# Attention stage of a three-stage language-model kernel: adjoining pairs on TensorE, one exponential per two heads, q and k stacked together

## The chip, the cores and the metric

The kernel runs on one NeuronCore of a Trainium2 chip. The metric is the device time of one execution in microseconds. Three runs of the kernel before took 1275.78, 1275.93 and 1276.22 us (median 1275.93).

## The reference

Three models run one after the other over 2048 tokens (8 sequences of 256) of width 256: a tower of four state-space layers, then an attention with a distance kernel, then two layers of windowed attention. Only the second is touched. On h, the layer-normed output of the tower:

```python
qh = (q @ Wq).reshape(Bq, Sq, H, D).transpose(0, 2, 1, 3)      # H = 16 heads of D = 16; k and v alike
q_norm = jnp.sum(qh * qh, axis=-1, keepdims=True)
qk = jnp.einsum('bhsd,bhtd->bhst', qh, kh)
dist = jnp.maximum(q_norm - 2.0 * qk + jnp.swapaxes(k_norm, -2, -1), 0.0)
scores = jnp.exp(-gamma[None, :, None, None] * SCALE * dist)
scores = jnp.where(mask, scores, 0.0)                          # mask: strictly above the diagonal
out = jnp.einsum('bhst,bhtd->bhsd', scores, vh)
return out.transpose(0, 2, 1, 3).reshape(Bq, Sq, H * D) @ Wo
```

## The kernel before

The second stage (`attention_phase`) handles one sequence of 256 tokens (two tiles t of 128) at a time, eight in all, M = 8. Products of fp32 accuracy are made of high and low parts: an engine rounds a value to fp32r (`_hi`), another subtracts it from the value (`_lo`), and TensorE multiplies the parts.

For a sequence s the steps are these. VectorE takes statistics and applies them twice (`norm_stats`, `norm_apply`, with k = 0 for the tower's last norm and k = 1 for the attention's own); GpSimd raises the variance to the power -1/2 (`rstd`) and applies scale and bias (`scale_h`, `bias_h`). TensorE transposes (`turn_x`), ScalarE and VectorE split (`spread`, `split_x`), TensorE projects (`project_qk`, one tile each, and `project_v`). ScalarE squares, VectorE sums per head (`norms`), and the two write a stacked row of 64 per head and tile: high and low parts of q, of -2k and of the norms, so that one product of 64 rows gives the whole distance (`query_hi`, `key_hi` on ScalarE, `stack` on VectorE). TensorE turns the rows (`turn`, eight transposes of 128x128 for q or k of one tile), ScalarE and, for the keys of tile 0, VectorE copy them out (`turned_q`, `turned_k`).

Then come eight pairs of heads, numbered 0 to 7. For a pair c TensorE computes `distances` (L938 and L941, four matmuls) into two banks, VectorE clips them at 0 (`clip`, L1336), ScalarE takes the exponential, one instruction per head since each head has its own factor `gsc` (`kernel_exp`, L1178), GpSimd masks (`mask`, L1476). After two pairs TensorE multiplies with the values (`values`, L959 and L957, quads 0 to 3 for pairs 0-1, 2-3, 4-5 and 6-7). `output_hi`, `output_lo`, `project_out` and `add_output` end the sequence.

All this is a software pipeline written out by hand. Each engine has a function `half(h)`, which lists what it does for several sequences at once, in fixed order; an engine works its list strictly in order and waits on semaphores. TensorE's half handles sequences a = h (projections of q and k), b = h-1 (values' projection, turns, the first two distances), c = h-2 (the other distances, values) and d = h-3 (output). VectorE's and GpSimd's lists are offset: the same stretch of time is their half h+3. Halves 2 to 8 of TensorE work on this stage alone; before them `first` and behind them halves 9 and 10 work beside the third stage, whose own halves follow.

The eight PSUM banks are shared by hand. The argument b of a step names a pair of banks, 2b and 2b+1 (`ps[:, 2 * b, ...]`).

In GpSimd's list two lines matter here: `rstd(c, 1)` (L1458) stands between `mask(f, 6)` and `mask(f, 7)`, and it waits for the `norm_stats(c, 1)` of VectorE (L1272, L1278, L1281).

## Time and profile before

| what | value |
|---|---|
| median of three runs | 1275.93 us |
| the profiled execution, own time | 1278.31 us |
| its span in the profile | 1276.4 us |
| TensorE busy | 1209.8 us, 95% |
| VectorE, ScalarE, GpSimd busy | 984.7, 860.2, 621.2 us |
| granted TensorE clock, mean over the span | 0.983 |
| second stage in the span | about 517 to 670 us |

Busy is the time an engine executes instructions; a matmul's end is modelled, so that starts of TensorE's instructions are to be read rather than their ends. A start-to-start time of two instructions is the price in a row of them; an instruction's own duration is a little longer, since the next one begins before it ends.

### The profile page before, as it was taken

Reading aid. Unit: us, or ns where it says so; the run is one execution under the profiler, and the core shown is the slowest. Engines: PE = TensorE matmul, PEld = TensorE weight load, DVE = VectorE, ACT = ScalarE, POOL = GpSimd, SP = SyncE. Lnnn points to the kernel's source line nnn. Section 1 sums busy time; section 2 is a strip of 40 time slices with the busy share of each in tenths; the row PEclk is TensorE's granted clock in tenths of the full one; section 3 lists DMA queues with packets and bytes.
Section 4 is the critical chain, followed back from the end, with each engine's and each line's share of the span. In section 5 each row is a group of like instructions: output and inputs, shape, how many; then the busy total and the mean of one; then the engine's idle time right before and its main releaser. Section 6 shows DMA issues by size and latency. Waiting matters only on the chain.

```text
span 1276.4 us, 26138 instructions
## 1 busy us (share of the span) xinstructions
PE 1209.8 (95%) x8899; PEld 1028.5 (81%) x8899; DVE 984.7 (77%) x2624; ACT 860.2 (67%) x1989; POOL 621.2 (49%) x678
## 2 busy tenths in 40 slices
PE   5999999999999999799978799999999999999998
PEld 3799988988888989577756567888888888888898
DVE  5767676666667777789878988888888888888754
ACT  2455766675556556689964668778777777777764
POOL 6523441361145243455434568556655567556543
PEclk9899999999999999899989999999999999999999
DMA  7400010001000000300110002000100000000001
GB/s 172 115 2 15 2 66 0 14 33 33 0 8 1 1 1 1 77 10 18 58 54 17 1 5 95 6 5 6 48 3 6 22 6 13 22 17 18 22 10 42
DMA packets 39615, 33.25 MB, mean 26 GB/s; under 512 B 16774, under 2 KB 36178, under 8 KB 39506
## 3 DMA queue, kind: packets, MB, share of 16 engines
q1 hardware_dynamic: 38610, 29.74, 7.7%
q0 software_dynamic: 768, 2.10, 1.0%
q8 instruction: 60, 0.98, 0.3%
q14 instruction: 49, 0.40, 0.1%
q10 hardware_dynamic: 128, 0.04, 0.0%
HBM read 25.84 MB, written 4.19 MB: 24 GB/s over the span
## 4 chain that ended last, share of the span: by engine, by line
PE 45%; DVE 6%; issue 3%; POOL 2%; ACT 2%; DVEq 0%; ACTq 0%; POOLq 0%
PE w_ps_p L1914 3%; PE w_ring L1975 3%; PE w_ring L1976 3%; PE w_ring L1873 3%; PE w_ring L1977 3%; PE w_ring L1875 3%; PE w_ring L1874 3%; PE w_ps_a L1932 2%; PE w_ring L1987 2%; PE a_ps L925 2%; PE w_ps_d L1907 2%; PE w_ps_d L1904 2%; PE w_ring L1891 2%; PE w_ring L1988 2%; PE w_ring L1991 1%
## 5 line engine op out<-in xcount | busy, mean ns | idle before, releaser
L392 ACT ACTIVATE t_gf<-t_ps_f,t_fb_cur 128x512 f32<-128x512 f32 x128 | 87.9, 687 | 159.8 <-PE t_ps_f L298 156.6
L542 DVE TENSOR_TENSOR t_g_lo<-t_gf,t_g_hi 128x512 fp32r<-128x512 f32 x128 | 93.3, 730 | 69.3 <-ACT t_g_hi L394 68.9
L311 PE MATMUL t_ps_o<-t_w_hi,t_g_hi 128*128 128x256 f32 x512 | 144.6, 282 | 0.1
L312 PE MATMUL t_ps_o<-t_w_lo,t_g_hi 128*128 128x256 f32 x512 | 143.0, 279 | 0.0
L313 PE MATMUL t_ps_o<-t_w_hi,t_g_lo 128*128 128x256 f32 x512 | 142.9, 279 | 0.0
L695 POOL TENSOR_TENSOR t_rs<-t_ve,t_neghalf 128x4 f32<-128x4 f32 x32 | 40.9, 1277 | 159.8 <-DVE t_ve L503 158.2
L296 PE MATMUL t_ps_f<-t_nh,t_w_hi 128*128 128x512 f32 x256 | 102.6, 401 | 1.5 <-DVE t_nl L518 0.8
L2988 POOL TENSOR_TENSOR w_m<-w_m 128x512 f32<-128x512 f32 x64 | 84.2, 1316 | 36.9 <-DVE w_m L2631 36.8
L298 PE MATMUL t_ps_f<-t_nl,t_w_hi 128*128 128x512 f32 x256 | 100.3, 392 | 0.0
L297 PE MATMUL t_ps_f<-t_nh,t_w_lo 128*128 128x512 f32 x256 | 100.0, 391 | 0.0
L311 PEld LDWEIGHTS t_ps_o<-t_w_hi,t_g_hi 128*128 128x128 f32 x512 | 96.2, 188 | 4.1 <-issue 0.9
L312 PEld LDWEIGHTS t_ps_o<-t_w_lo,t_g_hi 128*128 128x128 f32 x512 | 96.7, 189 | 2.5
L313 PEld LDWEIGHTS t_ps_o<-t_w_hi,t_g_lo 128*128 128x128 f32 x512 | 96.8, 189 | 0.0
L2674 DVE COPY w_pt<-w_ps_p 128x384 f32<-128x384 f32 x128 | 70.5, 551 | 31.4 <-PE w_ps_p L1914 29.9
L1975 PE MATMUL w_ring<-w_nh,w_w_hi 128*128 128x256 f32 x318 | 93.5, 294 | 0.0
L1976 PE MATMUL w_ring<-w_nh,w_w_lo 128*128 128x256 f32 x318 | 88.8, 279 | 0.0
L1977 PE MATMUL w_ring<-w_nl,w_w_hi 128*128 128x256 f32 x318 | 88.7, 279 | 0.0
L2999 POOL TENSOR_TENSOR w_pr<-w_pr,w_rinv 128x256 f32<-128x256 f32 x64 | 39.3, 614 | 101.0 <-DVE w_rinv L2668 101.0
L1873 PE MATMUL w_ring<-qkv_hi,w_ah 128*128 128x512 f32 x188 | 80.6, 429 | 6.7 <-DVE w_al L2613 5.7
L3004 POOL TENSOR_TENSOR w_h_lo<-w_gate,w_h_hi 128x256 fp32r<-128x256 f32 x75 | 54.6, 737 | 60.1 <-ACT w_h_hi L2413 60.1
L394 ACT ACTIVATE t_g_hi<-t_gf 128x512 fp32r<-128x512 f32 x128 | 80.9, 632 | 4.1
L1178 ACT ACTIVATE a_e<-a_dist,a_gsc 128x384 f32<-128x384 f32 x128 | 70.2, 621 | 8.3 <-DVE a_dist L1336 6.8
(369 smaller groups left out, 4285.0 us busy)
## 6 DMA issues: line engine op xcount, KB each, us to landing
t_raw<-in_L_tok_w SPq DMA_DIRECT2D x8, 1024.0 KB, 5.4
out<-X SPq DMA_DIRECT2D x14, 256.0 KB, 2.2
raw<-in_L_ffn_wqkv SPq DMA_DIRECT2D x2, 1536.0 KB, 6.9
raw<-in_L_ffn_w SPq DMA_DIRECT2D x4, 640.0 KB, 4.8
w_raw_o<-out SPq DMA_DIRECT2D x8, 256.0 KB, 2.8
w_xs<-X SPq DMA_DIRECT2D x14, 127.0 KB
w_raw<-in_L_ffn_w SPq DMA_DIRECT2D x2, 640.0 KB
t_raw_d<-in_L_tok_D SPq DMA_DIRECT2D x4, 256.0 KB
```

The source lines that it names most:

```text
L296: pe.matmul(ps_f[:, j % 2, :], w1_hi[:, c, col], nh[1][:, c, :], start=(c == 0), stop=False)
L297: pe.matmul(ps_f[:, j % 2, :], w1_lo[:, c, col], nh[1][:, c, :], start=False, stop=False)
L298: mm = pe.matmul(ps_f[:, j % 2, :], w1_hi[:, c, col], nl[1][:, c, :], start=False, stop=(c == DC - 1))
L311: pe.matmul(out, g_hi[:, j % 4, tok], w2_hi[:, j, :], start=(j == 0 and t % 2 == 0), stop=False, skip_group_check=True)
L312: pe.matmul(out, g_hi[:, j % 4, tok], w2_lo[:, j, :], start=False, stop=False, skip_group_check=True)
L313: mm = pe.matmul(out, g_lo[:, j % 4, tok], w2_hi[:, j, :], start=False, stop=(j == FC - 1 and t % 2 == 1), skip_group_check=True)
L392: act.activation(gf[:, j % 2, :], ps_f[:, j % 2, :], ACT.Gelu, bias=fb_cur[:, j:j + 1]).then_inc(pf_free, 1)
L542: dve.tensor_tensor(g_lo[:, j % 4, :], gf[:, j % 2, :], g_hi[:, j % 4, :].bitcast(F32), ALU.subtract).then_inc(g_split, 1)
L1873: pe.matmul(ring[:, RB[b], :], ah[:, c, tok], qkv_hi[:, c, cols], start=(c == 0), stop=False)
L1975: pe.matmul(dst, w1_hi[:, c, u, cols], n_hi[:, c, :], start=(j % 2 == 0 and c == 0), stop=False, skip_group_check=True)
L1976: pe.matmul(dst, w1_lo[:, c, u, cols], n_hi[:, c, :], start=False, stop=False, skip_group_check=True)
L1977: mm = pe.matmul(dst, w1_hi[:, c, u, cols], n_lo[:, c, :], start=False, stop=(j == chunks[-1] and c == DC - 1), skip_group_check=True)
```

## The change

On TensorE, `distances` of pairs 3 and 4, 6 and 7, and 0 and 1 of the next sequence stand side by side, and so do the values of quads 0 and 1, and 2 and 3. The banks are shared out anew: pair 1's distances go to banks 1 and 2 (`MID`), the projection of q and k to one bank named directly (0 and 3), the output to bank 3 (2 for the last two sequences). The turns of q and k of a tile adjoin. The clip takes the minimum of the negated half distance and 0 and multiplies by `gsc` in the same instruction, so that one exponential of 768 columns serves two heads, without a factor. q and k lie in one tile `qk`: one ScalarE instruction of 512 columns writes the high parts of both (two for the first sequence), GpSimd writes the second copy (`stack_twin`), and VectorE needs three instructions in place of six for a stack. `turned_k(·, 0)` moves from VectorE to ScalarE. On VectorE, `norm_stats` and `norm_apply` stand at other places.

The diff, cut to its core:

```diff
+        def pair(t, q_at, k_at, n):
+            apart = KEYS + k_at - q_at
+            both = qk[t][:, q_at:q_at + 2 * apart].rearrange("p (i w) -> p i w", i=2)
+            return both[:, :, 0:H * ROW].rearrange("p i (h r) -> p i h r", r=ROW)[:, :, :, 0:n]
...
@@ tensor, half
                 if real(b):
                     pe.wait_ge(v_done, 2 * b + 2)
                     turn(b, 0, 0, 2)
+                    if real(c):
+                        pe.wait_ge(relu_done, 8 * c + 3)
...
+                    turn(b, 0, 1, 0)
                 if real(c):
...
                     distances(c, 3, 1)
...
                     distances(c, 4, 3)
                 if real(b):
+                    pe.wait_ge(qt_done, 2 * b + 1)
+                    turn(b, 1, 0, 2)
...
                     values(c, 0, 2)
+                    values(c, 1, 2)
                     pe.wait_ge(relu_done, 8 * c + 5)
                     distances(c, 6, 3)
-                    values(c, 1, 2)
                     pe.wait_ge(relu_done, 8 * c + 6)
                     distances(c, 7, 0)
...
-                    project_out(d, 1)
+                    project_out(d, out_bank(d))
...
                     distances(b, 0, 3)
+                    if real(c):
+                        pe.wait_ge(relu_done, 8 * c + 8)
+                    pe.wait_ge(kt_done[1], b + 1)
+                    distances(b, 1, MID)
...
                     project_qk(a, 0, 0)
-                if real(b):
-                    pe.wait_ge(relu_done, 8 * b + 1)
-                    distances(b, 1, 3)
-                if real(c):
+                if real(c):
+                    values(c, 2, 2)
                     values(c, 3, 2)
...
-                    project_qk(a, 1, 1)
+                    project_qk(a, 1, 3)
@@ scalar
+            def stack_hi(s, t, b):
...
+                both = ps[:, b, :].rearrange("p (i h d) -> p i h d", i=2, d=HD)
+                if s == 0:
+                    act.activation(pair(t, HD, 2 * HD, HD), both, ACT.Copy).then_inc(twin, 1)
+                act.activation(pair(t, 0, 0, HD), both, ACT.Copy).then_inc(qk_hi, 1)
...
-                for x in range(2):
-                    h = 2 * c + x
-                    ins = act.activation(e[:, h % SLOTS, :], dist[:, h % BANKS, :], ACT.Exp, scale=gsc[:, h:h + 1])
-                ins.then_inc(exp_done, 1)
+                h = 2 * c
+                act.activation(e[:, h % SLOTS:h % SLOTS + 2, :], dist[:, h % BANKS:h % BANKS + 2, :], ACT.Exp).then_inc(exp_done, 1)
@@ vector
-                dve.tensor_scalar(dist[:, two, :], ps[:, 2 * b:2 * b + 2, 0:SCORES], 0.0, None, ALU.max).then_inc(relu_done, 1)
+                rate = gsc[:, 2 * c:2 * c + 2].unsqueeze(2).broadcast_to([P, 2, SCORES])
+                dve.scalar_tensor_tensor(dist[:, two, :], ps[:, two_banks(b), 0:SCORES], 0.0, rate, ALU.min, ALU.mult).then_inc(relu_done, 1)
@@ vector, half
+                if real(f):
+                    clip(f, 5, 0)
                 if real(b):
                     norm_apply(b, 0)
-                if real(f):
-                    clip(f, 5, 0)
-                if real(c):
-                    norm_stats(c, 1)
                 if real(f):
                     clip(f, 6, 3)
                     clip(f, 7, 0)
...
-                if real(a):
-                    norm_stats(a, 0)
                 if real(e):
                     clip(e, 0, 3)
                 if real(g):
-                    add_output(g, 1)
-                if real(c):
-                    norm_apply(c, 1)
+                    add_output(g, out_bank(g))
+                if real(c):
+                    norm_stats(c, 1)
+                if real(e):
+                    clip(e, 1, MID)
                 if real(f):
                     output_lo(f, 0, 2)
-                if real(e):
-                    clip(e, 1, 3)
+                if real(a):
+                    norm_stats(a, 0)
                 if real(d):
                     norms(d, 0)
                 if real(f):
                     output_lo(f, 1, 2)
+                if real(c):
+                    norm_apply(c, 1)
                 if real(d):
                     stack(d, 0, 0)
-                    norms(d, 1)
-                    stack(d, 1, 1)
                 if real(e):
                     clip(e, 2, 0)
+                if real(d):
+                    norms(d, 1)
+                    stack(d, 1, 3)
+                if real(c):
+                    split_x(c, 6)
+                if real(e):
                     clip(e, 3, 1)
-                if real(c):
-                    split_x(c, 6)
-                if real(d):
-                    turned_k(d, 0, 0)
-                if real(e):
                     clip(e, 4, 3)
@@ gpsimd
+            def stack_twin(s, t):
+                pool.wait_ge(qk_hi, 2 * s + t + 1)
+                pool.tensor_copy(pair(t, HD, 2 * HD, HD), pair(t, 0, 0, HD).bitcast(F32)).then_inc(twin, 1)
```

In `half` of GpSimd, `stack_twin(e, 1)` follows `bias_h(c)`, and `stack_twin(d, 0)` follows `mask(e, 0)`. `mask(f, 6)`, `rstd(c, 1)`, `mask(f, 7)` stay as they stood.

VectorE, in a half of the middle (all sequences real), from the clip of pair 5 to `add_output` (L1345, now L1344). `a_dist` is the clip, `a_xn` is `norm_apply`, `a_st`, `a_mv` and `a_ve` are `norm_stats`. Before:

```order
L1288 TENSOR_SCALAR a_xn<-X,a_mv,a_rs 128x256 [waits a_h_mul,a_rs0]
L1288 TENSOR_SCALAR a_xn<-X,a_mv,a_rs 128x256
L1336 TENSOR_SCALAR a_dist<-a_ps 128x768 [waits a_exp,a_d_full]
L1272 BN_STATS a_st<-X 128x6 [waits a_h_ready]
L1272 BN_STATS a_st<-X 128x6
L1278 BN_AGGR a_mv<-a_st 128x2 [waits a_xn1,a_st1]
L1278 BN_AGGR a_mv<-a_st 128x2
L1281 TENSOR_SCALAR a_ve<-a_mv 128x2 [waits a_mv1]
L1336 TENSOR_SCALAR a_dist<-a_ps 128x768 [waits a_exp,a_d_full] x2
```

and now:

```order
L1335 SCALAR_TENSOR_TENSOR a_dist<-a_ps,a_gsc 128x768 [waits a_exp,a_d_full] x3
L1344 TENSOR_TENSOR X<-a_ps,X 128x512 [waits a_y_full]
L1276 BN_STATS a_st<-X 128x6 [waits a_h_ready]
L1276 BN_STATS a_st<-X 128x6
L1282 BN_AGGR a_mv<-a_st 128x2 [waits a_xn1,a_st1]
L1282 BN_AGGR a_mv<-a_st 128x2
L1285 TENSOR_SCALAR a_ve<-a_mv 128x2 [waits a_mv1]
L1335 SCALAR_TENSOR_TENSOR a_dist<-a_ps,a_gsc 128x768 [waits a_exp,a_d_full]
```

The statistics whose variance is `a_ve1` stood behind the clip of pair 5, ahead of pairs 6 and 7. They now stand behind the clips of pairs 6 and 7 and of pair 0 of the next sequence (the row with x3), and behind `add_output`.

GpSimd, the same half, from its masks of pairs 2 to 4 on. `a_e` is `mask`, `a_rs` is `rstd`. Before:

```order
L1476 AFFINE_SELECT a_e<-a_e 128x2x256 [waits a_exp] x3
L1464 TENSOR_TENSOR X<-a_xn,a_fs 128x512 [waits a_xn0]
L1476 AFFINE_SELECT a_e<-a_e 128x2x256 [waits a_exp] x2
L1458 TENSOR_TENSOR a_rs<-a_ve,a_neghalf 128x2 [waits a_ve1]
L1476 AFFINE_SELECT a_e<-a_e 128x2x256 [waits a_exp] x2
L1458 TENSOR_TENSOR a_rs<-a_ve,a_neghalf 128x2 [waits a_ve0]
```

and now:

```order
L1474 AFFINE_SELECT a_e<-a_e 128x2x256 [waits a_exp] x3
L1462 TENSOR_TENSOR X<-a_xn,a_fs 128x512 [waits a_xn0]
L1474 AFFINE_SELECT a_e<-a_e 128x2x256 [waits a_exp] x2
L1456 TENSOR_TENSOR a_rs<-a_ve,a_neghalf 128x2 [waits a_ve1]
L1474 AFFINE_SELECT a_e<-a_e 128x2x256 [waits a_exp] x2
L1479 CAST a_qk<-a_qk 128x2x16x16 [waits a_qk_hi]
L1456 TENSOR_TENSOR a_rs<-a_ve,a_neghalf 128x2 [waits a_ve0]
```

Ahead of the mask of pair 7 (first of the x2 behind `a_rs`) stands the power that waits for `a_ve1`, as before; only the cast is new.

TensorE, from the distances of pair 5 to the output's first matmul. Before:

```order
L938 MATMUL a_ps<-a_qt,a_kt 128x256 x2
L941 MATMUL a_ps<-a_qt,a_kt 128x128 x2
L959 MATMUL a_ps<-a_e,a_v 32x256 x4
L957 MATMUL a_ps<-a_e,a_v 32x128 x4
L938 MATMUL a_ps<-a_qt,a_kt 128x256 x2
L941 MATMUL a_ps<-a_qt,a_kt 128x128 x2
L959 MATMUL a_ps<-a_e,a_v 32x256 x4
L957 MATMUL a_ps<-a_e,a_v 32x128 x4
L938 MATMUL a_ps<-a_qt,a_kt 128x256 x2
L941 MATMUL a_ps<-a_qt,a_kt 128x128 x2
L968 MATMUL a_ps<-wa_ohi,a_ot_hi 128x256
```

and now:

```order
L959 MATMUL a_ps<-a_qt,a_kt 128x256 x2
L962 MATMUL a_ps<-a_qt,a_kt 128x128 x2
L980 MATMUL a_ps<-a_e,a_v 32x256 x4
L978 MATMUL a_ps<-a_e,a_v 32x128 x4
L980 MATMUL a_ps<-a_e,a_v 32x256 x4
L978 MATMUL a_ps<-a_e,a_v 32x128 x4
L959 MATMUL a_ps<-a_qt,a_kt 128x256 x2
L962 MATMUL a_ps<-a_qt,a_kt 128x128 x2
L959 MATMUL a_ps<-a_qt,a_kt 128x256 x2
L962 MATMUL a_ps<-a_qt,a_kt 128x128 x2
L989 MATMUL a_ps<-wa_ohi,a_ot_hi 128x256
```

The matmuls are the same; values adjoin values and distances adjoin distances.

## Rows read from the trace of the kernel before

**Rows 1.** Page, part 1: busy time of each engine
```profile
PE 1209.8 (95%) x8899; PEld 1028.5 (81%) x8899; DVE 984.7 (77%) x2624; ACT 860.2 (67%) x1989; POOL 621.2 (49%) x678
```
**Rows 2.** TensorE in order of time, one full half: start, us, line, shapes, [idle before]
```profile
592.05 0.39 PE L938 MATMUL a_ps<-a_qt,a_kt 64*128 64x256 f32 x2
...
596.36 0.39 PE L938 MATMUL a_ps<-a_qt,a_kt 64*128 64x256 f32 x2
...
597.18 0.64 PE L959 MATMUL a_ps<-a_e,a_v 128*32 128x256 f32 x8 [0.38 <-POOL a_e L1476]
...
599.98 0.64 PE L959 MATMUL a_ps<-a_e,a_v 128*32 128x256 f32 x8
...
602.28 0.28 PE L899 MATMUL a_ps<-wa_whi,a_nh 128*128 128x256 f32 x1
...
608.68 1.09 PE L925 MATMUL a_ps<-a_ident,a_ks 128*128 128x128 f32 x8
...
609.71 0.39 PE L938 MATMUL a_ps<-a_qt,a_kt 64*128 64x256 f32 x2
```
**Rows 3.** VectorE in order of time, the same half
```profile
594.13 0.74 DVE L1272 BATCH_NORM_STATS2 a_st<-X 128x6 f32<-128x256 f32 x2
...
595.18 0.17 DVE L1281 TENSOR_SCALAR a_ve<-a_mv 128x2 f32<-128x2 f32 x1
...
597.48 0.96 DVE L1336 TENSOR_SCALAR a_dist<-a_ps 128x768 f32<-128x768 f32 x1 [0.40 <-ACT a_e L1178]
598.35 0.68 DVE L1345 TENSOR_TENSOR X<-a_ps,X 128x512 f32<-128x512 f32 x1
```
**Rows 4.** GpSimd and ScalarE in order of time, the same half
```profile
596.25 1.12 ACT L1178 ACTIVATE a_e<-a_dist,a_gsc 128x384 f32<-128x384 f32 x2 [0.69 <-DVE a_dist L1336]
...
598.05 0.71 POOL L1458 TENSOR_TENSOR a_rs<-a_ve,a_neghalf 128x2 f32<-128x2 f32 x1
599.29 0.64 POOL L1476 TENSOR_SCALAR_AFFINE_SELECT a_e<-a_e 128x512 f32<-128x512 f32 x1 [0.53 <-ACT a_e L1178]
```
**Rows 5.** Groups of instructions by form: busy us, mean ns, idle before
```profile
L445 ACT ACTIVATE wa_whi<-raw 128x768 fp32r<-128x768 f32 x2 | 1.7, 853 | 0.0
L173 POOL CAST t_d_hi<-t_raw_d 128x512 fp32r<-128x512 f32 x3 | 1.8, 612 | 0.0
L1328 DVE CAST a_kt<-a_ps 128x1024 fp32r<-128x1024 f32 x8 | 9.7, 1215 | 5.8 <-PE a_ps L925 5.8
L1300 DVE TENSOR_REDUCE a_nrm<-a_sq 128x32 f32<-128x512 f32 x16 | 10.9, 679 | 2.7 <-ACT a_sq L1131 2.5
```
**Rows 6.** TensorE in order of time, two distances that adjoin in the last halves
```profile
651.93 0.38 PE L938 MATMUL a_ps<-a_qt,a_kt 64*128 64x256 f32 x2
...
652.21 0.33 PE L938 MATMUL a_ps<-a_qt,a_kt 64*128 64x256 f32 x2
```
**Rows 7.** TensorE in order of time: pair 5's distances of halves 2, 3, 7 and 9
```profile
536.42 0.39 PE L938 MATMUL a_ps<-a_qt,a_kt 64*128 64x256 f32 x2
...
556.73 0.38 PE L938 MATMUL a_ps<-a_qt,a_kt 64*128 64x256 f32 x2
...
626.88 0.39 PE L938 MATMUL a_ps<-a_qt,a_kt 64*128 64x256 f32 x2
...
653.93 0.39 PE L938 MATMUL a_ps<-a_qt,a_kt 64*128 64x256 f32 x2 [1.10 <-DVE a_dist L1336]
```
**Rows 8.** TensorE in order of time, two idle gaps of the third stage
```profile
906.26 0.55 PE L1914 MATMUL w_ps_p<-w_ident,w_pr 128*128 128x128 f32 x3 [1.44 <-POOL w_pr L3000]
...
1082.62 0.65 PE L1932 MATMUL w_ps_a<-w_pt,w_v 128*64 128x256 f32 x4 [1.80 <-issue]
```
**Rows 9.** Busy time by stretch, with granted clock behind POOL's busy time
```profile
543.00:544.00 1.00, 1.00 (x7) 0.81 (x4) 1.00 (x3) 1.00 (x4) 0.47 (x2) 0.50 0.00 0
...
906.00:910.00 4.00, 3.74 (x27) 2.89 (x28) 2.92 (x7) 1.56 (x5) 2.74 (x4) 1.00 0.93 330
...
1083.00:1085.00 2.00, 2.00 (x14) 1.59 (x11) 2.00 (x9) 0.38 (x1) 2.00 (x4) 0.64 0.04 8
```

More of the change, by code:

```diff
@@ L803, in attention_phase @@
     PARTS = 8
+    MID = -1
     with ExitStack() as ctx:
@@ L828, in attention_phase @@
         nrm = [sb(f"nrm{t}", [P, 2 * H]) for t in range(ST)]
-        qs = [sb(f"qs{t}", [P, H, ROW], F32R) for t in range(ST)]
-        ks = [sb(f"ks{t}", [P, H, ROW], F32R) for t in range(ST)]
+        KEYS = (H + 1) * ROW
+        qk = [sb(f"qk{t}", [P, 2 * KEYS + ROW], F32R) for t in range(ST)]
         v = sb("v", [P, 2 * ST, H, 2 * HD])
@@ L904, in project_qk @@
             def project_qk(s, t, b):
-                project(t, ps[:, 2 * b, :], 0, 2 * D, qk_full)
+                project(t, ps[:, b, :], 0, 2 * D, qk_full)
             def project_v(s, t, b):
@@ L1111, in first @@
                 pe.wait_ge(kt_done[0], 1)
+                pe.wait_ge(kt_done[1], 1)
+                distances(0, 1, MID)
                 project_qk(1, 0, 0)
-                pe.wait_ge(relu_done, 1)
-                distances(0, 1, 3)
-                pe.wait_ge(kt_done[1], 1)
-                project_qk(1, 1, 1)
+                project_qk(1, 1, 3)
             return half, opening, first
@@ L1440, in opening @@
                     norms(0, 1)
-                    stack(0, 1, 1)
+                    stack(0, 1, 2)
                     norm_apply(2, 0)
@@ L1487, in half @@
                     bias_h(c)
+                if e > 0 and real(e):
+                    stack_twin(e, 1)
                 if 0 <= g < PARTS // 2:
@@ L1507, in half @@
                     mask(e, 0)
+                if d > 0 and real(d):
+                    stack_twin(d, 0)
                 if real(a):
```

106 lines of the change are left out of this document (43 added, 63 removed).

## The prediction

> **What bounds the kernel now.** I read the page first: TensorE is busy 95% of the span, VectorE 77% [rows 1]. Then I read the second stage in order of time, engine by engine, since the change lies in it alone. TensorE's full halves there are alike. I measure one from its distances of pair 5 to the next: 592.05 to 609.71, 17.66 us [rows 2]. In it TensorE waits little: 0.38 us for a mask ahead of the third values, and fractions elsewhere. The row of that wait is what the reader should see: TensorE has some 17 us of work, and VectorE, with its statistics, clips and stacks in a row, is nearly as full. So an engine's work comes off the time only if no order of waits grows in its place.
>
> **ScalarE.** A pair's two exponentials take 1.12 us to be done [rows 4]. One of 768 columns has no row; a copy of 768 columns takes 0.853 [rows 5], and one instruction can hardly take longer than the two it replaces. I take 0.85 and keep 1.12 as the other end. High parts of q and k: four instructions of 256 columns become one of 512. The turned keys of tile 0 come over from VectorE. All in all ScalarE gets some 2 us freer in a half. It stands behind the clips, not ahead of them, so that in a full half this is cover and not gain; I cost it at nothing there. If it failed (1.12 again), ScalarE would be as full as before, not fuller.
>
> **VectorE** loses the key copy, 1.215 us [rows 5], and about 0.15 per stack. The clip has the same 768 columns read from PSUM; its start-to-start time stays at 0.87 (597.48 to 598.35 [rows 3]). A second input from SBUF could cost nothing or a tenth; I take nothing.
>
> **GpSimd** gets two casts of 128x512, 0.612 us each [rows 5]. The one of tile 1 stands ahead of the masks of pairs 2 and 3. Laid out in time, the mask of pair 3 is then done about 0.65 us after pair 5's distances start, and the second values want it at 1.0. The other is in time by more. If they took 1.3 us (the upper bound, a 512-column operation with two inputs there), they would still be just in time.
>
> The page "GPSIMD Engine Reference" of the Trainium skill (Specifications) says that GpSimd shares its SBUF interface with VectorE's two-port and two-input instructions, which speaks against work put on GpSimd. Nothing in the sum would change by it: VectorE's new stack and clip read PSUM beside one SBUF input.
>
> **TensorE** has the same matmuls. A pair's distances take 0.37 us among other work, and 0.28 when another's follow (651.93 to 652.21 [rows 6]). Three adjoinings and fewer switches to and from values give up to 0.7 us of a half. That is the most a full half can gain, with the waits that vanish: down to about 16.1.
>
> **The wait that the change adds.** The mask of pair 7 stands on GpSimd behind the power of `rstd(c, 1)`, and that waits for `norm_stats(c, 1)`. Before, the statistics began at 594.13 and their last instruction at 595.18 [rows 3], long before the power at 598.05 [rows 4]. Now they stand behind the clip of the next sequence's pair 0 and behind `add_output`, so behind TensorE's output projection. What is late is the fourth values and all that TensorE has behind them: the second projection of q and k, the values' projections, the transposes. With pair 5's distances as zero:
> - Next sequence's pair 0 distances: 4.31 before (596.36), 4.03 now, one switch and one adjoining less.
> - To its clip 0.48 (four matmuls and their drain), clip 0.87, `add_output` 0.60 (598.35 [rows 3] less the overlap).
> - Statistics 1.22 (594.13 to the end of the row at 595.18, which lasts 0.17 [rows 3]).
> - Power and mask: 0.05 for the signal, 0.62 and 0.64 (rows of 0.71 and 0.64 [rows 4]), 0.05 again.
> - Fourth values at 8.56, where they stood at 7.93 (599.98 [rows 2]). TensorE is ready for them at 6.83, by its own work. It stands 1.7 us.
> - From them to the next half 2.30 (to 602.28 [rows 2]): 10.86.
>
> From there to pair 5's distances it was 7.43 (609.71). Now the transposes for the next sequence start at 1.6, pair 2's distances at 2.2, and VectorE clips them from 2.7 to 3.6. Then come `norms` and the stack's first subtraction, 0.60 each start to start (both run over 512 columns; the row for `norms` has 0.679 [rows 5]), done at 4.85: pair 3's distances wait 0.28 for that. Two small instructions and `split_x` (512 columns too) are done at 5.76, and pair 4's distances wait 0.65 for that. Two turns of eight at 1.0 each (608.68 to 609.71 [rows 2]) and 0.37 lead to 8.15. The full half takes **19.0 us** in place of 17.66.
>
> **The sum.**
> - Up to pair 5 of half 2: `norm_stats(2, 1)` now waits for the first clip, and the turns of tile 1 for GpSimd's cast behind the third stage's masks: +1.35.
> - Half 2 took 20.31 (536.42 to 556.73 [rows 7]), since TensorE's clock was at its lower level, 0.50, in part of it (543 to 544 [rows 9]). The same walk, with no output to project, gives 18.1: -2.2.
> - Halves 3 to 6 took 70.15 (556.73 to 626.88 [rows 7]); four at 19.0 are 76.0: +5.85.
> - Halves 7 and 8 took 27.05 (626.88 to 653.93 [rows 7]). They have no such statistics, so here the freed time shows: TensorE's own work with small waits, 15.8 and 8.5: -2.75.
> - The rest: exponentials stand in the chain twice, at 0.27 saved each: -0.5.
>
> Together +1.75 us, with the clock as it was.
>
> **The clock.** A gap of 1.7 us in every full half may bring it down. In the third stage a gap of 1.80 us (before 1082.62) was followed by a granted clock of 0.64 from 1083 to 1085, so by 1.2 GHz in most of that time; one of 1.44 (before 906.26) by 1.00 from 906 to 910, 2.4 GHz [rows 8, 9]. I take a fall to last 4 us, in which 2 us of TensorE's work are lost, all of it behind the late values, where TensorE leads. I take two of the four halves as hit: +4.0; none and all are the ends, 0 and +8.
>
> The sum is +5.75 on the profiled execution's own 1278.31 us, 1284.1. That execution lies 2.4 us above the median of the runs, 1275.93; against the median the forecast is **1281.6 us**.
>
> **Rivals.**
> - *A, the forecast*, 0.40: late mask, clock down in some halves, 1281.6.
> - *B, the clock holds*, 0.24: the same waits, +1.75: 1277.7. For it: 1.44 us left the clock up. Here the page "TensorE: Matmul & The Clock Gate" (Why this matters for your kernels) comes in: by it only gaps longer than any that I forecast bring the clock down. The row of 1.80 us speaks against that, so it gets less than A.
> - *C, every full half is hit*, 0.10: the clock falls in halves 2 to 6, +1.75 + 10: 1287.7. For it: 536 to 557 shows that half 2 can be hit at smaller gaps.
> - *D, faster*, 0.26: the lightened VectorE reaches the statistics and the split earlier than my walk says. It is decided in a full half, at the fourth values and at pair 4's distances: if the first wait is 0.7 and the second nothing, a half takes 17.35, and four of them 69.4. Then -0.85 - 0.75 - 3.25 = -4.85: 1271.1. Below 18.2 us for a full half the kernel is faster than before, the clock holding. Against it: the statistics can't start before the output's projection is through, however fast VectorE is.
> - The change may not do what it says, if one exponential costs as much as two. Halves 7 to 10 then keep some 1.5 us of their 3.25. It is inside the range of A to C and has no chance of its own.
>
> **How the numbers follow.** A change of 0.2%, 2.55 us, is about what a measurement here can tell from none. A and C are slower by more: 0.50, and 0.02 of B with them, 0.52. The rest of B is within, 0.22. D is faster, 0.26. The range from 1270.5 to 1287 holds A, B, most of D and half of C: 8 in 10 once the errors of a walk are allowed for.
>
> **What would show it.** GpSimd's `a_rs` row of each full half (L1456) should have idle time before it, ended by `a_ve` of VectorE, and TensorE's fourth values (L980) some 1.7 us ended by the mask. A full half should take 19 us, halves 7 and 8 together 24. The exponential should show 0.85 us, the clip 0.95, the cast 0.6 to 0.7. The clock should be at 0.5 in stretches behind the late values. I am wrong if the fourth values don't wait, or if a full half comes below 18.2 us.

## The result and the profile after

The changed kernel took **1290.47 us** (median of four runs, 1289.62 to 1291.93), the kernel before 1275.86 beside it. The ratio is 1.0122, with a 95% interval from 1.0103 to 1.0141: slower by 1.2%. The forecast was 1281.6, with a range up to 1287.0, so the direction was right and the size outside the range. The profiled execution of the changed kernel had 1290.0 us of its own and a span of 1287.9, 11.5 us more than that of before.

Part 1 of the page, busy time of each engine, beside [rows 1]:

```profile
PE 1207.4 (94%) x8899; PEld 1028.0 (80%) x8899; DVE 978.7 (76%) x2567; ACT 843.8 (66%) x1886; POOL 628.8 (49%) x692
```

Every engine but GpSimd has less to do than before: VectorE 6 us, ScalarE 16 us (843.8 for 860.2), TensorE 2.4 us. With a span 11.5 us longer, TensorE's idle time grew by 13.9 us. I took the same marks from both traces. TensorE's distances of pair 5 (those of half 2, of half 3, of half 7 and of half 9), and the first projection of the third stage, in order of time, as in [rows 7]:

```profile
539.22 0.38 PE L959 MATMUL a_ps<-a_qt,a_kt 64*128 64x256 f32 x2
...
558.50 0.39 PE L959 MATMUL a_ps<-a_qt,a_kt 64*128 64x256 f32 x2
...
639.37 0.39 PE L959 MATMUL a_ps<-a_qt,a_kt 64*128 64x256 f32 x2
...
664.72 0.43 PE L959 MATMUL a_ps<-a_qt,a_kt 64*128 64x256 f32 x2 [0.63 <-DVE a_dist L1335]
...
677.22 0.50 PE L1879 MATMUL w_ring<-qkv_hi,w_ah 128*128 128x512 f32 x1 [1.62 <-DVE w_al L2619]
```

| stretch | before | forecast | after |
|---|---|---|---|
| first distances to pair 5 of half 2, with 0.75 us that stood before it | 11.28 | 12.6 | 14.08 |
| half 2 | 20.31 | 18.1 | 19.28 |
| halves 3 to 6 | 70.15 | 80.0 (4.0 of it clock) | 80.87 |
| halves 7 and 8 | 27.05 | 24.3 | 25.35 |
| from there to the third stage's first projection | 14.77 | 14.3 | 12.50 |
| behind that | | 0 | +3.0 |

The first five lines make +8.5 us, the last +3.0. (A forecast cell is the value of before plus the forecast's term.)

**A full half** took 20.1 us where 19.0 were forecast. TensorE in order of time, from pair 5's distances of one half to the next (start, us, line, [idle before, what ended it]):

```profile
600.25 0.38 PE L959 MATMUL a_ps<-a_qt,a_kt 64*128 64x256 f32 x2
...
608.89 0.64 PE L980 MATMUL a_ps<-a_e,a_v 128*32 128x256 f32 x8 [1.58 <-POOL a_e L1474]
...
611.18 0.28 PE L918 MATMUL a_ps<-wa_whi,a_nh 128*128 128x256 f32 x1
...
613.38 0.38 PE L959 MATMUL a_ps<-a_qt,a_kt 64*128 64x256 f32 x2
...
616.08 0.39 PE L959 MATMUL a_ps<-a_qt,a_kt 64*128 64x256 f32 x2
...
618.06 0.39 PE L959 MATMUL a_ps<-a_qt,a_kt 64*128 64x256 f32 x2 [1.54 <-DVE a_nl L1297]
...
620.33 0.39 PE L959 MATMUL a_ps<-a_qt,a_kt 64*128 64x256 f32 x2
```

The fourth values (608.89) wait 1.58 us for the mask of pair 7, at 8.64 behind pair 5's distances (forecast 8.56; 7.93 before [rows 2]). Pair 4's distances (618.06) wait 1.54 us for `split_x` (forecast 0.65). From the values' projection to the next pair 5 it is 9.15, not 8.15. GpSimd shows the first of the two waits as forecast: the power stands 1.89 us for `a_ve`, and the mask of pair 7 is the first of the two behind it.

```profile
607.52 0.71 POOL L1456 TENSOR_TENSOR a_rs<-a_ve,a_neghalf 128x2 f32<-128x2 f32 x1 [1.89 <-DVE a_ve L1285]
608.20 1.24 POOL L1474 TENSOR_SCALAR_AFFINE_SELECT a_e<-a_e 128x512 f32<-128x512 f32 x2
...
614.54 1.28 POOL L1467 TENSOR_TENSOR X<-X,a_fb 128x512 f32<-128x512 f32 x1
615.77 0.61 POOL L1479 CAST a_qk<-a_qk 128x512 fp32r<-128x512 f32 x1
616.34 1.95 POOL L1483 TENSOR_TENSOR qkv_lo<-raw,qkv_hi 128x384 fp32r<-128x384 f32 x2
```

VectorE, the same half, in front of `split_x` (L1297):

```profile
613.88 0.96 DVE L1335 SCALAR_TENSOR_TENSOR a_dist<-a_ps,a_gsc 128x768 f32<-128x768 f32 x1 [1.61 <-ACT a_e L1184]
614.75 0.68 DVE L1304 TENSOR_REDUCE a_nrm<-a_sq 128x32 f32<-128x512 f32 x1
615.34 0.68 DVE L1312 TENSOR_TENSOR a_qk<-a_ps,a_qk 128x512 fp32r<-128x512 f32 x1
615.94 0.50 DVE L1317 CAST a_qk<-a_nrm 128x32 fp32r<-128x32 f32 x1
616.48 0.93 DVE L1319 TENSOR_TENSOR a_qk<-a_nrm,a_qk 128x32 fp32r<-128x32 f32 x1
617.33 0.68 DVE L1297 TENSOR_TENSOR a_nl<-a_ps,a_nh 128x512 fp32r<-128x512 f32 x1
```

Up to 615.94 all is where the walk put it: clip at 2.70 behind the values' projection (2.7), subtraction done at 4.76 (4.85). Then come two instructions of 32 columns, which the walk gave 0.3 us together. They took 1.4. In the first stack of the same half (611.82 and 612.05) they took 0.20 and 0.22, with GpSimd idle. Here the first ends at 616.44, and GpSimd's cast at 616.38; the second ends at 617.41, and the first of the two `qkv_rest`, half of the row of 1.95, at about 617.3. Meanwhile L1312, which reads PSUM and SBUF, kept its 0.68 beside `bias_h`, which ran to 615.82.

**The clock.** It fell in only one of the halves 3 to 6, at pair 4's distances at 576.36, for which TensorE had waited 1.59 us. In half 2, where it was down in the trace of before, it did not fall. The busy times by stretch, granted clock third from the right, of the kernel before and of the changed one:

```profile
540.00:548.00 8.00, 6.96 (x47) 4.01 (x48) 6.09 (x13) 5.44 (x13) 4.77 (x7) 0.57 0.00 0
656.00:668.00 12.00, 9.28 (x72) 6.14 (x72) 8.12 (x21) 5.73 (x13) 4.38 (x6) 0.57 0.12 34
...
696.00:700.00 4.00, 3.27 (x18) 2.27 (x19) 2.79 (x17) 2.63 (x12) 1.61 (x2) 1.00 0.01 2
...
709.00:713.00 4.00, 3.79 (x20) 3.17 (x21) 3.83 (x15) 1.73 (x6) 1.61 (x2) 1.00 0.00 0
```

```profile
577.00:580.00 3.00, 3.00 (x18) 2.96 (x16) 1.05 (x2) 1.86 (x2) 0.83 (x2) 0.57 0.00 0
...
664.00:670.00 6.00, 4.39 (x49) 2.30 (x46) 5.82 (x14) 3.12 (x5) 3.58 (x5) 0.72 0.75 235
...
705.00:709.00 4.00, 3.74 (x14) 2.37 (x14) 1.62 (x10) 2.15 (x10) 1.61 (x2) 0.61 0.00 0
...
719.00:723.00 4.00, 3.72 (x11) 3.02 (x12) 2.77 (x13) 0.96 (x4) 1.61 (x2) 0.57 0.00 0
```

Up to the third stage the kernel before lost 3.4 us of full-speed work in half 2 (8.0 times 0.43) and 5.2 at the end; the changed one lost 1.3 and 1.7. Behind it, it is the other way. The third stage's first halves are the same instructions in both, and its waits up to there differ by 0.01 us, yet the changed kernel has 0.61 from 705 to 709 and 0.57 from 719 to 723, 1.6 and 1.7 us lost, where the kernel before has 1.00 at the same place of its program (696 to 700, 709 to 713). That is the +3.0, to within 0.3: the distance between the two traces grows from 8.5 us (696.73 and 705.26) to 10.1 (709.21 and 719.28) and 11.6 (716.69 and 728.33), one step at each of the two. Why the clock fell there in one trace and not in the other stays open. From 748.09 in the trace of before, 759.54 in that of after, all 32 additions to X keep their distance of 11.2 to 11.5 us.

### The profile page after: what moved, and what is told of

Its sections match the earlier page's. It is cut to its first block, busy times and chain, and to the rows that moved or that the text cites. A ratio compares the mean times of both kernels' runs of the same rounds, so it can differ in the third digit from the quotient of the medians.

```text
span 1287.9 us, 25995 instructions
## 1 busy us (share of the span) xinstructions
PE 1207.4 (94%) x8899; PEld 1028.0 (80%) x8899; DVE 978.7 (76%) x2567; ACT 843.8 (66%) x1886; POOL 628.8 (49%) x692
## 4 chain that ended last, share of the span: by engine, by line
PE 46%; DVE 6%; issue 3%; POOL 2%; ACT 2%; DVEq 0%; ACTq 0%; POOLq 0%
PE w_ps_p L1920 3%; PE w_ring L1879 3%; PE w_ring L1981 3%; PE w_ring L1881 3%; PE w_ring L1982 3%; PE w_ring L1983 3%; PE w_ring L1880 3%; PE w_ps_a L1938 2%; PE w_ring L1993 2%; PE w_ps_d L1913 2%; PE w_ring L1897 2%; PE w_ps_d L1910 2%; PE a_ps L945 2%; PE w_ring L1994 2%; PE w_ring L1997 1%
## 5 line engine op out<-in xcount | busy, mean ns | idle before, releaser
L1335 DVE SCALAR_TENSOR_TENSOR a_dist<-a_ps,a_gsc 128x768 f32<-128x768 f32 x64 | 59.7, 953 | 24.5 <-PE a_ps L962 22.4
```

## The experiments

Each is timed against runs of the kernel before on the same chip (4, 18, 20 or 23 runs); a ratio is taken over all runs and can differ a little from that of the two medians. "Stage" is the time from the second stage's first distances to the third stage's first projection in the profiled execution (before 143.6, changed 151.3).

| label | median us | ratio to before (95%) | full half us | stage us |
|---|---|---|---|---|
| changed | 1290.5 | 1.0122 (1.0103 to 1.0141) | 20.1 | 151.3 |
| a_power | 1281.4 | 1.0044 (1.0023 to 1.0064) | 18.3 | 145.0 |
| a_stack | 1284.8 | 1.0062 (1.0037 to 1.0088) | 18.8 | 149.9 |
| a_both | 1288.8 | 1.0108 (1.0071 to 1.0146) | 20.0 | 152.4 |
| a_rest | 1284.3 | 1.0069 (1.0045 to 1.0092) | 19.6 | 150.7 |
| a_early | 1290.0 | 1.0102 (1.0070 to 1.0134) | 20.4 | 155.4 |
| b_late | 1284.8 | 1.0063 (1.0043 to 1.0083) | 18.7 to 19.5 | 147.6 |
| b_late_pw | 1278.1 | 1.0007 (0.9991 to 1.0023) | 17.6 to 18.1 | 141.8 |
| b_exp | 1275.3 | 0.9999 (0.9984 to 1.0013) | 18.0 to 18.3 | 139.3 |
| b_lock | 1279.0 | 1.0028 (1.0012 to 1.0044) | 17.9 | 142.5 |
| p_clear | 1276.4 | 0.9997 (0.9983 to 1.0011) | 17.4 to 18.3 | 139.2 |
| p_best | 1278.7 | 1.0021 (1.0008 to 1.0034) | 18.1 to 18.4 | 143.0 |
| p_stats | 1274.2 | 0.9975 (0.9962 to 0.9988) | 17.4 | 136.8 |

Falls of the clock differ from run to run, and the time goes with them: of the 18 runs of the kernel before beside a_power, the eight with a granted clock of 0.983 took 1277.7 to 1280.0 us, the seven with 0.989 to 0.991 took 1271.3 to 1274.3. The full half is taken from halves 3 to 5, where the clock stayed up (in a_early and a_both it fell in every one), and says more of an order of instructions than the total does.

### The two late links, alone and together

**a_power**, GpSimd:

```diff
-                if real(c):
-                    rstd(c, 1)
                 if real(f):
                     mask(f, 7)
+                if real(c):
+                    rstd(c, 1)
```

> The changed kernel with one exchange on GpSimd: the power rstd(c, 1) goes behind the mask of pair 7. Theory (two late links, each of some 1.55 us a half: the mask of pair 7 held back by the late statistics, and split_x late for pair 4's distances): the fourth values lose their wait (1.58 in four halves, 0.79 in one, 7.1 us in all) and nothing takes its place, pair 4's distances still wait 1.5 each; a full half falls from 20.1 to about 18.5 and the time from 1290.5 to about 1283.5. Rival 1 (the statistics themselves are the lateness; the wait moves on to the transposes of x, which need norm_apply(c, 1)): the same 1.5 us appear ahead of the transposes, no gain over 2 us, about 1289. Rival 2 (the loss is the clock's: fewer gaps, fewer falls): more than 9 us, below 1281, with a granted clock of 1.00 throughout stage two.

9 us gained (1290.5 to 1281.4), and not one of the fourth values of halves 2 to 6 waits: the exchange of two lines on GpSimd is worth more than half the loss. Pair 4's distances still wait, 0.88 or 1.6 us. A wait of 0.66 us for the second `output_lo` is new. The gain beyond the 7.1 us of waits lies within what the clock does, so neither rival is needed.

**a_stack**, VectorE:

```diff
-                if real(e):
-                    clip(e, 2, 0)
                 if real(d):
                     norms(d, 1)
                     stack(d, 1, 3)
+                if real(e):
+                    clip(e, 2, 0)
```

> The changed kernel with norms(d, 1) and stack(d, 1) back ahead of the clip of pair 2 on VectorE. Theory: VectorE's idle 1.6 us ahead of that clip is used, split_x is done by about 615.8 in place of 618.0 in the half of 600 to 620, and the wait of pair 4's distances (1.54 to 1.59 us in four halves, 1.38 and 0.51 in two, 8.2 us in all) goes; the clip of pair 2 comes about 0.3 us later, of which the keys' turns feel up to 0.3. The mask's wait of 1.58 stays. Gain 6 to 8 us: about 1283.5. Rival (the lateness is VectorE's whole load and only moves to the clip of pair 2 or to the keys' turns): less than 3 us gained, about 1289, with a wait of over 1 us at pair 3's distances or the turns.

1284.8, near the theory's 1283.5. The wait at pair 4's distances is gone and the mask's stays (1.58 to 1.59 us); the keys' turns wait for the clip, 0.2 us in the halves of 18.8 us, 0.52 in half 3 (19.1) and 2.05 in half 2.

**a_both**, both edits:

> Both exchanges in one kernel. Theory: two independent links in a row on TensorE's path, so the gains add: 14 us, about 1276.5, a full half 17.0 to 17.3, level with the kernel before within 0.3%. Rival (they are one bound, seen at two places: relieving one moves the wait to the other): the gain of both is hardly more than that of the better one, about 1283.

The gains do not add: 1288.8, worse than either, and my theory was wrong. TensorE, then VectorE and GpSimd, in order of time:

```profile
593.35 1.09 PE L945 MATMUL a_ps<-a_ident,a_qk 128*128 128x128 f32 x8 [2.25 <-DVE a_dist L1335]
```

```profile
590.35 0.68 DVE L1312 TENSOR_TENSOR a_qk<-a_ps,a_qk 128x512 fp32r<-128x512 f32 x1
590.94 0.24 DVE L1317 CAST a_qk<-a_nrm 128x32 fp32r<-128x32 f32 x1
591.22 1.21 DVE L1319 TENSOR_TENSOR a_qk<-a_nrm,a_qk 128x32 fp32r<-128x32 f32 x1
592.35 0.94 DVE L1335 SCALAR_TENSOR_TENSOR a_dist<-a_ps,a_gsc 128x768 f32<-128x768 f32 x1
...
591.10 1.26 POOL L1467 TENSOR_TENSOR X<-X,a_fb 128x512 f32<-128x512 f32 x1
```

The room that a_stack used ahead of the clip of pair 2 was there because the late mask held TensorE back: VectorE stands idle for 1.61 us before that clip in the changed kernel (613.88), and for 0.28 with the mask in time (571.57 in a_power). With the mask in time, the whole stack stands in front of a clip for which TensorE's turns of the keys wait, 2.25 us. Behind gaps of 2.04 to 2.26 us the clock fell in three halves. The 16 turns of tile 1 took 3.60 us in the half of 20.0, 1.99 with the clock up, so that some 1.6 us of it are the clock's doing. Even without them the half would be no shorter than a_power's 18.3. One of VectorE's small instructions takes 1.21 us there. It ends at 592.43, and `bias_h` on GpSimd (L1467) at 592.36.

**a_early**, VectorE:

```diff
+                if real(c):
+                    norm_stats(c, 1)
                 if real(f):
                     clip(f, 6, 3)
...
-                if real(c):
-                    norm_stats(c, 1)
```

> The changed kernel with the other cure of the mask's wait: norm_stats(c, 1) back on VectorE ahead of the clips of pairs 6 and 7 (behind norm_apply(b, 0)), GpSimd as in the change. Theory (late statistics hold the power, and it the mask): the fourth values lose their 1.58 us, as with the power moved. But the statistics, 1.2 us, now stand ahead of two clips that TensorE wants for its next distances: some 0.6 to 0.8 us of wait at pair 6's or pair 0's distances per half. Gain 4 to 5 us, about 1286, so less than the 9 us of the exchange on GpSimd. Rival (VectorE has room for them there): 1281, like the exchange.

The mask's wait went, but nothing was gained. `split_x` stayed late (1.5 to 1.6 us in every half up to 5, 0.52 behind it), and the next sequence's pairs 0 and 1 waited for clips (2.59 and 0.42 us in half 2, 1.05 and 0.42 in half 3, then 0.28 at pair 1). The clock was down in part of each half from 2 to 6 (the 16 turns at 579.51: 2.87 us in place of 1.97), some 1.7 us of work each. Without that a half of 20.4 would be one of some 18.7 (an estimate from these two numbers), so the order by itself seems to save and the clock took it back. That the order brought the falls on isn't shown.

### The late statistics in the kernel before

**b_late** puts `norm_stats(c, 1)` behind `add_output` and `norm_apply(c, 1)` behind the second `output_lo`:

```diff
-                if real(c):
-                    norm_stats(c, 1)
                 if real(f):
                     clip(f, 6, 3)
...
                 if real(g):
                     add_output(g, 1)
                 if real(c):
-                    norm_apply(c, 1)
+                    norm_stats(c, 1)
...
                     output_lo(f, 1, 2)
+                if real(c):
+                    norm_apply(c, 1)
```

> The kernel before with one thing of the change: norm_stats(c, 1) behind add_output, and norm_apply(c, 1) behind the second output_lo. Theory: the late statistics alone cost the kernel before 1.4 to 1.6 us at the fourth values in each of four full halves and 0.8 in half 2, since the mask of pair 7 waits behind the power there too: 6 to 8 us, about 1283.5. Rival (in the kernel before VectorE is later anyway, and TensorE reaches the fourth values only when the mask is there): under 2 us, 1278.

8 us slower with these two steps late, and the wait stands at the fourth values, 1.0 to 1.85 us in halves 2 to 6:

```profile
584.40 0.64 PE L959 MATMUL a_ps<-a_e,a_v 128*32 128x256 f32 x8 [1.84 <-POOL a_e L1476]
```

**b_late_pw** adds the exchange of a_power to it:

> The kernel before with the statistics late (1284.8 us) and, on GpSimd, the power behind the mask of pair 7. Theory (what costs is the mask's place in GpSimd's list, not the late statistics as such): the waits of 1.0 to 1.85 us at the fourth values go and the time falls by 6 to 8 us, 1277 to 1279. Rival (norm_apply and the transposes are late as well): the transposes of x wait 1 us, 1281 to 1283.

1278.1, level with the kernel before in the same runs. The statistics may be late; the mask of pair 7 may not stand behind their power. Together with a_power this shows the first wait's cause from both sides.

### GpSimd and VectorE's small instructions

The trace of the kernel before has such a row already, in the third stage. VectorE's 128x16 instruction, 0.177 us in the median of 32, takes 1.22 and ends at 684.58, GpSimd's at 684.54:

```profile
683.36 1.22 DVE L2647 SCALAR_TENSOR_TENSOR w_yb<-w_ya,w_sc 128x16 f32<-128x16 f32 x1
...
683.25 1.29 POOL L2988 TENSOR_TENSOR w_m<-w_m 128x512 f32<-128x512 f32 x1
```

**a_rest**, GpSimd:

```diff
-                if 0 <= g < PARTS // 2:
-                    qkv_rest(2 * g)
-                    qkv_rest(2 * g + 1)
...
                     mask(f, 4)
+                if 0 <= g < PARTS // 2:
+                    qkv_rest(2 * g)
+                    qkv_rest(2 * g + 1)
```

> The changed kernel with GpSimd's two qkv_rest of a half behind the masks of pairs 2 to 4 in place of ahead of them. VectorE's two small instructions of a stack (32 columns) took 0.50 and 0.93 us beside GpSimd's cast and qkv_rest in four halves, against 0.20 and 0.22 where GpSimd stood still. Theory (the two engines hold each other up at SBUF): they fall to 0.2 to 0.5 and 0.2, split_x comes 0.7 to 1.0 us earlier, the wait at pair 4's distances goes from 1.55 to 0.6 to 0.9 in four halves, gain 3 to 4 us, about 1287. Rival (the length is a wait or the instruction's own, the write to two far apart places of the row): no change in either row, 1290.5.

Pair 4's distances wait 0.86 in place of 1.55, as forecast:

```profile
596.42 0.39 PE L959 MATMUL a_ps<-a_qt,a_kt 64*128 64x256 f32 x2 [0.86 <-DVE a_nl L1297]
```

One size was missed: `qkv_rest` in the new place delays the masks of pairs 5 to 7, and the third values now wait 0.5 us. So the half got only 0.5 shorter, some 2 us in all. The median is 6 us lower, but six of the seven runs had a granted clock of 0.986 to 0.991, the four of the changed kernel 0.982 to 0.985; the profiled run of a_rest, with 0.983, took 1289.6. So most of the rest seems to go with the clock.

**b_lock** puts the two `qkv_rest` of the kernel before ahead of `mask(e, 1)`, into GpSimd's idle time:

> The kernel before with one thing moved: GpSimd's two qkv_rest of a half ahead of the mask of pair 1, where GpSimd is idle (4 us) and VectorE has the small instructions of its stacks, which read SBUF alone (0.17 to 0.19 us each). In the kernel before they run beside clips and splits, which read PSUM. Theory (such an instruction stands until GpSimd's running one ends): in four halves one or two of the small ones take 0.4 to 1.0 us, each ending within 0.1 us of the end of a qkv_rest, while the 256-column instructions from PSUM between them keep 0.41; the clip of pair 2 comes 0.5 to 1 us later in four halves, of which TensorE feels 0.3 to 0.8: 1 to 3 us, 1278 to 1279. Rival (the long rows of the changed kernel come from its new form, two far apart places in one tile): all small ones keep 0.17 to 0.19, 1276.6.

The ratio of 1.0028 is small but clear of 1. GpSimd and VectorE in order of time:

```profile
585.73 2.01 POOL L1481 TENSOR_TENSOR qkv_lo<-raw,qkv_hi 128x384 fp32r<-128x384 f32 x2
...
586.33 0.46 DVE L1309 CAST a_qs<-a_nrm 128x16 fp32r<-128x16 f32 x1
...
586.77 0.41 DVE L1314 TENSOR_TENSOR a_qs<-a_ps,a_qs 128x256 fp32r<-128x256 f32 x1
587.11 0.40 DVE L1316 SCALAR_TENSOR_TENSOR a_ks<-a_ps,a_ks 128x256 fp32r<-128x256 f32 x1
587.44 0.35 DVE L1318 TENSOR_TENSOR a_qs<-a_nrm,a_qs 128x16 fp32r<-128x16 f32 x1
```

L1309 ends at 586.79, the first `qkv_rest`, half of the row of 2.01, at about 586.74; L1318 at 587.79, the second at 587.74. The two from PSUM between them take what they always take, with GpSimd busy all along. The longest L1309 of this run has 1049 ns, where its median is 186. So it is not the changed kernel's new form.

**b_exp**, the kernel before with the clip and the exponential of the change:

```diff
-                dve.tensor_scalar(dist[:, two, :], ps[:, 2 * b:2 * b + 2, 0:SCORES], 0.0, None, ALU.max).then_inc(relu_done, 1)
+                rate = gsc[:, 2 * c:2 * c + 2].unsqueeze(2).broadcast_to([P, 2, SCORES])
+                dve.scalar_tensor_tensor(dist[:, two, :], ps[:, 2 * b:2 * b + 2, 0:SCORES], 0.0, rate, ALU.max, ALU.mult).then_inc(relu_done, 1)
...
-                for x in range(2):
...
+                act.activation(e[:, h % SLOTS:h % SLOTS + 2, :], dist[:, h % BANKS:h % BANKS + 2, :], ACT.Exp).then_inc(exp_done, 1)
```

> The kernel before with one exponential per two heads alone (the factor goes into the clip, which becomes a scalar_tensor_tensor with a second input from SBUF). The prediction costed it at nothing in full halves and -0.5 us in all: exponential 0.84 us in place of 1.12, clip 0.95 in place of 0.94, time within 1 us of the kernel before, 1276. Rival (the exponentials stand on the path of the masks and values more often): 2 to 4 us faster, 1273.

The total is that of before, the durations are as forecast (0.847 and 0.948 us). But it is not mere cover: a half with its output took 18.26 us, not 17.6, since the first distances of the next sequence wait 0.73 for a clip. VectorE and GpSimd there:

```profile
573.51 1.21 DVE L1277 TENSOR_SCALAR a_ve<-a_mv 128x2 f32<-128x2 f32 x1
574.63 1.81 DVE L1333 SCALAR_TENSOR_TENSOR a_dist<-a_ps,a_gsc 128x768 f32<-128x768 f32 x2
...
573.40 1.29 POOL L1462 TENSOR_TENSOR X<-a_xn,a_fs 128x512 f32<-128x512 f32 x1
```

A 128x2 instruction of the statistics (0.17 us as a rule) takes 1.21. With the masks of pairs 4 and 5 earlier, `scale_h` now runs beside it and ends at 574.69, the other at 574.72. Why the median stayed level all the same isn't shown. The profiled execution, which lies 1.9 us below it, had no fall of the clock between 523 and 663, where that of before lost 8.6 us of work; nothing here says that the new exponential brought that about.

### Towards a version that holds

**p_clear**, on top of a_power: `stack_twin(d, 1)` ahead of `mask(e, 1)`, `bias_h` behind `mask(f, 2)`, the two `qkv_rest` behind `mask(f, 3)`.

> The changed kernel with the power behind the mask of pair 7 (1281.4 us alone), and GpSimd's other work moved out of the time of VectorE's small instructions: stack_twin(d, 1) ahead of the mask of pair 1, bias_h behind the mask of pair 2, qkv_rest behind the mask of pair 3. Theory (a small VectorE instruction that reads SBUF alone stands until GpSimd's running instruction ends: 591.22 + 1.21 ends at 592.43, bias_h at 592.36 in the kernel with both exchanges; 592.25 + 0.52 ends at 592.77, the cast at 592.71 in the one with the power alone): both take 0.2 in every half, pair 4's distances wait 0.4 to 0.7 in place of 0.88 and 1.65. But the same must then happen to norm_apply(b, 0), which reads SBUF alone too and now runs beside qkv_rest: 0.2 to 0.7 us later clips of pairs 6 and 7. Net 1279 to 1281. Rival (only slower execution in part, by shared bandwidth): small ones at 0.3 and more whatever stands beside them.

1276.4, level with before and 5 us better than a_power. All 16 of L1319 are short now, which in a_power went up to 936 ns:

```profile
L1319 DVE TENSOR_TENSOR a_qk<-a_nrm,a_qk x16: 216/220/225, 503.2 to 640.9; 128x32 fp32r<-128x32 f32 x16
```

And the price that the theory asked for is there: `norm_apply(b, 0)`, two instructions beside `qkv_rest`, takes 1.18 us in place of 0.73 in three halves. Pair 4's distances wait 0.52.

**p_best** added to p_clear the second `output_lo` and `norm_apply(c, 1)` ahead of `norms(d, 0)`, the stack of tile 1 in two around `split_x`, and, at the start, pair 1's distances behind `project_qk(1, 0)`.

> The kernel with the power moved and GpSimd cleared (1276.4 us), and on VectorE three more places: the second output_lo and norm_apply(c, 1) ahead of norms(d, 0), so that the second v projection loses its 0.66 us and the transposes their 0.15; stack(d, 1) in two, with split_x between the subtraction that reads PSUM and the two small instructions, so that pair 4's distances lose most of their 0.52 us in five halves; and at the start pair 1's distances behind project_qk(1, 0), so that their 1.21 us go. Theory (TensorE's path is short waits on VectorE's order, and nothing else is behind them): 2 + 2 + 1 us, 1271 to 1272, 0.4% faster than the kernel before, a full half 16.9 to 17.1 in place of 18.2 and 17.5. Rival (VectorE is full at this point, the waits move to pair 3's distances or the keys' turns): 1275 to 1276, no gain.

The rival came: 1278.7 us, 2.3 above p_clear (on another chip, where the kernel before had 1275.1 and not 1276.7; by the ratios it is 3 us). Each wait that I aimed at shrank, and three others came: 0.45 at pair 2's distances, 0.42 at the turns of tile 1, 0.30 at the first values. The small instruction, moved behind `split_x`, met GpSimd's mask, and ended at 588.22, the mask at 588.14:

```profile
587.55 0.67 DVE L1326 TENSOR_TENSOR a_qk<-a_nrm,a_qk 128x32 fp32r<-128x32 f32 x1
...
587.50 0.64 POOL L1482 TENSOR_SCALAR_AFFINE_SELECT a_e<-a_e 128x512 f32<-128x512 f32 x1 [2.35 <-ACT a_e L1184]
```

**p_stats** took work out of the crowded stretch instead, again on top of p_clear; the two `qkv_rest` leave their place behind `mask(f, 3)`:

```diff
+                if b > 3 and real(b):
+                    norm_stats(b, 0)
                 if real(f):
                     clip(f, 5, 0)
...
-                if real(a):
-                    norm_stats(a, 0)
@@ gpsimd
+                if 0 <= g < PARTS // 2:
+                    qkv_rest(2 * g)
                 if real(f):
                     mask(f, 2)
...
+                if b > 3 and real(b):
+                    rstd(b, 0)
                 if real(f):
                     mask(f, 4)
+                if 0 <= g < PARTS // 2:
+                    qkv_rest(2 * g + 1)
...
-                if real(a):
-                    rstd(a, 0)
```

> The kernel with the power moved and GpSimd cleared (1276.4 us), and 1.2 us of VectorE's work taken out of the stretch between the next sequence's first clip and pair 4's distances: norm_stats(a, 0) goes into the idle time (1.09 us) ahead of the clip of pair 5 of the next half, rstd(a, 0) on GpSimd with it, behind the mask of pair 3; the two qkv_rest stand ahead of the mask of pair 2 and behind that of pair 4. Theory (what is left on TensorE's path are VectorE's last 0.5 us ahead of split_x and 0.66 at the second output_lo, and both come from VectorE being full in this stretch): both waits go, a full half takes 16.9 to 17.2 us, the time is 1272 to 1273.5, faster than the kernel before by 0.2 to 0.3%. Rival (as with the reordered stack: the moved instructions meet GpSimd's and stretch, or the clip of pair 5 comes late for the values' banks): 1276 or above.

1274.2 against 1278.25 in the same runs, ratio 0.9975: faster than both kernels, by 0.1 to 0.4% of the one before. Part of it is the clock: 12 of the 23 runs of the kernel before had 0.983 there, and no run of p_stats was below 0.985. The wait at the second `output_lo` went. That at pair 4's distances stayed at 0.52, where what is late seems to be not VectorE as a whole but the chain behind pair 2's distances (read from the order, not tested). TensorE, pair 4's distances of halves 3 to 5:

```profile
552.67 0.39 PE L959 MATMUL a_ps<-a_qt,a_kt 64*128 64x256 f32 x2 [0.52 <-DVE a_nl L1297]
...
570.10 0.39 PE L959 MATMUL a_ps<-a_qt,a_kt 64*128 64x256 f32 x2 [0.52 <-DVE a_nl L1297]
...
587.54 0.38 PE L959 MATMUL a_ps<-a_qt,a_kt 64*128 64x256 f32 x2 [0.51 <-DVE a_nl L1297]
```

17.4 us a half, against 17.66 before and 20.1 in the change.

## Why the prediction was wrong in size and right in direction

- **The mask of pair 7**: right. At 8.64 (8.56 forecast), 1.58 us (1.7), in the places named, ended by the `a_ve` named; b_late and a_power show that it is this wait, and with some 8 us of 14.6 it is the greater part of the loss.
- **`split_x` and pair 4's distances**: the step that failed. "Two small instructions and `split_x` ... are done at 5.76, and pair 4's distances wait 0.65": done at 6.8, a wait of 1.54 to 1.59. I priced the two by rows in which GpSimd stood idle, and didn't lay GpSimd's `bias_h`, cast and `qkv_rest` beside them. a_rest, b_lock and p_clear show that this overlap is the difference; in p_clear, without it, the wait is 0.52. The clip of pair 2, which the change put ahead of the second stack, moved them into it. Worth 1.1 us in each of halves 3 to 5, and most likely the 1.2 us by which half 2 missed (19.28 for 18.1; the same wait of 1.59 stands in it at 556.24). Half 6 has no `qkv_rest`, and there the walk holds: 19.04 us, 19.0 forecast.
- **The rule that I waved off.** The prediction said that sharing an SBUF interface changes nothing, because the new stack and clip read PSUM. It looked at the big new instructions and not at the small old ones. The page "SBUF — State Buffer" of the Trainium skill (SBUF: two separate sides) is sharper: the pair of ports is an exclusive lock for a whole instruction, and whoever comes second is blocked, a VectorE instruction with two SBUF inputs among them. The rows agree: the seven stretched instructions read above, from 616.44 in the changed kernel to 588.22 in p_best, end 0.03 to 0.1 us behind GpSimd's, and three of them have one SBUF input only. The trace of before had the price (683.36).
- **Up to pair 5 of half 2**: forecast +1.35, measured +2.05 in that stretch and 0.75 already ahead of it. Pair 4's distances wait 1.38 us for `split_x` there, which the walk of half 1 left out. What made the 0.75 is not known.
- **Halves 7 and 8**: -1.7 where -2.75 was forecast; the waits at the last clips stayed.
- **The clock**: +4.0 was forecast for halves 3 to 6; one fall cost 1.5. There the two errors, 3.4 too little and 2.5 too much, nearly cancel. In the end region it helped (-2.3 in all, with less of the clock lost), and in the opening of the third stage it cost +3.0, which no step of mine had in view. Without that last the profiled execution would be near 1287.
- **From the profiled execution to the median.** The forecast took off 2.4 us, the distance of the profiled execution of before from its median. That execution had a granted clock of 0.983, at which all runs of this kernel beside the experiments took 1277.7 us or more; its distance looks to be the clock's, and the sum had already taken the fall of half 2 out once, with the -2.2. The changed kernel's profiled execution (0.985) lies 0.5 below its median. That makes 2.9 us of the miss.
- **The miss as a whole** is 8.9 us (1290.5 for 1281.6), of which these terms, rounded, make 8.7: +1.45 up to pair 5 of half 2, +1.2 in half 2, +0.9 in halves 3 to 6, +1.05 in halves 7 and 8, -1.8 behind them, +3.0 in the third stage, +2.9 by the median. The direction was right by its mechanism; that the miss was no larger is luck in part, since `split_x` and the clock went opposite ways in halves 3 to 6.
- **ScalarE as cover**: right in the total (b_exp), wrong as a mechanism there: earlier masks pulled `scale_h` onto a VectorE instruction. In the changed kernel the exponential (0.84), the clip (0.96) and the cast (0.61) cost what was said, and the mask of pair 3 was in time.

## What to carry to other kernels

Before you move an instruction of VectorE that has all its operands in SBUF, however small, look at what GpSimd runs in the new place, and charge it with the rest of that instruction. A wait written ahead of an unrelated step in an in-order list costs as soon as its producer moves; here the cure was to exchange two lines on the consumer's engine. And slack seen beside a wait may be the wait's own doing: test cures together, not only one by one.
